# ScalarE's order of the layer-2 copies, GpSimd's order of gathers, TensorE's order of layer-2 pairs, in a three-layer interaction network on one core

## What is computed

```
xk = relu(einsum('bmd,bhd,mhk->bkd', x0, xk, W))     # W0: 32x32x64, W1 and W2: 32x64x64
outs.append(sum(xk, axis=2))
```

## Time and profile before

| | us |
|---|---|
| median of 3 runs | 665.63 |
| lowest, highest | 664.72, 666.06 |
| the profiled execution | 662.89 |
| its span | 661.1 |
| PE busy in the span | 605.5 (92%) |
| DVE busy | 569.6 (86%) |
| POOL busy | 453.1 (69%) |
| ACT busy | 358.0 (54%) |

### The profile page before, as it was taken

How to read it: one execution, slowest core, us unless ns; L and a number is a source line. 1 busy time by engine, 2 the same in 40 slices (tenths; PEclk the granted TensorE clock), 3 DMA queues, 4 the chain that set the end, 5 groups by cost and what they waited for, 6 DMA issues and landing times. The chain is left out here.

```text
span 661.1 us, 9151 instructions
## 1 busy us (share of the span) xinstructions
PE 605.5 (92%) x3172; PEld 247.5 (37%) x3172; DVE 569.6 (86%) x336; ACT 358.0 (54%) x669; POOL 453.1 (69%) x307
## 2 busy tenths in 40 slices
PE   4499849979999999989999999999999999999988
PEld 3352313224343344424343344434443443434434
DVE  5759975986989899897989899898989898999863
ACT  0184922817647392927647392928556482829251
POOL 6786887888869694888869697787877070716220
PEclk9689969989999999999999999999999999999989
DMA  6899679797695969698694969688795869492000
GB/s 186 190 240 278 150 213 214 217 216 193 146 248 142 208 199 214 193 200 237 141 255 137 213 193 211 193 198 225 180 258 131 186 217 217 155 214 41 1 0 1
DMA packets 60175, 119.82 MB, mean 181 GB/s; under 512 B 15271, under 2 KB 33734, under 8 KB 60054
## 3 DMA queue, kind: packets, MB, share of 16 engines
q1 hardware_dynamic: 41798, 111.02, 67.1%
q10 hardware_dynamic: 10768, 6.53, 3.7%
q0 software_dynamic: 7584, 1.96, 3.0%
HBM read 115.27 MB, written 5.25 MB: 182 GB/s over the span
## 5 line engine op out<-in xcount | busy, mean ns | idle before, releaser
L483 DVE TENSOR_TENSOR z_dve<-xq,x0b 128x2048 f32<-128x2048 f32 x209 | 464.5, 2283 | 68.4 <-ACT xq L637 39.2
L879 PE MATMUL acc<-z_dve,w_cin 128*64 128x512 f32 x1672 | 379.2, 597 | 11.1 <-DVE z_dve L483 10.8
L439 POOL TENSOR_TENSOR z_pool<-x0b,xs 128x2048 f32<-128x2048 f32 x47 | 213.5, 4558 | 108.2 <-ACT xs L637 107.2
L423 POOL DMA_INDIRECT emb<-in_tbl_dram,ids_all x224 | 220.0, 982 | 72.0 <-issue 70.3
L879 PEld LDWEIGHTS acc<-z_dve,w_cin 128*64 128x64 f32 x1672 | 122.4, 137 | 234.9 <-issue 186.5
L645 ACT ACTIVATE xq<-acc 32x512 f32<-32x512 f32 x256 | 144.6, 565 | 3.4
L637 ACT ACTIVATE xq<-acc 64x512 f32<-64x512 f32 x128 | 73.0, 570 | 119.8 <-DVE z_dve L483 62.8
L879 PE MATMUL acc<-z_pool,w_cin 128*64 128x512 f32 x376 | 90.6, 615 | 16.1 <-POOL z_pool L439 16.1
L637 ACT ACTIVATE xs<-acc 64x512 f32<-64x512 f32 x128 | 75.7, 591 | 1.9
L483 DVE TENSOR_TENSOR z_dve<-xq,x_rot 128x2048 f32<-128x2048 f32 x30 | 67.2, 2281 | 0.0
L879 PE MATMUL acc<-z_dve,w_sym 128*64 128x512 f32 x256 | 58.0, 593 | 0.2 <-DVE z_dve L483 0.2
(11 more groups left out here) (97 smaller groups left out, 229.2 us busy)
## 6 DMA issues: line engine op xcount, KB each, us to landing
x0b<-x0t SPq DMA_DIRECT2D x120, 512.0 KB, 14.5
x_rot<-x0t SPq DMA_DIRECT2D x60, 512.0 KB, 6.2
x_rep<-x0t SPq DMA_DIRECT2D x15, 512.0 KB
x0b<-x0t SPq DMA_DIRECT2D x16, 256.0 KB, 7.2
emb<-in_tbl_dram,ids_all POOLq DMA_INDIRECT x224
x0t<-emb_t ACTq DMA_DIRECT2D x28, 128.0 KB
w_cin<-in_L_rec_W_dram SPq DMA_DIRECT2D x16, 64.0 KB
x_lo<-x0t SPq DMA_DIRECT2D x15, 64.0 KB
```

What stands on the lines that cost most here:

```text
L423: nc.gpsimd.indirect_dma_start(out=rows[:, D * f:D * f + D], out_offset=None, in_=tables[f], in_offset=bass.IndirectOffsetOnAxis(ap=ids_al ...
L439: nc.gpsimd.tensor_tensor(z_pool[:, n % ZP_SLOTS, :, :], x0b[b % 2][:, 2 * j:2 * j + 2, :], xs[l - 1][:, :].unsqueeze(1).broadcast_to([P, ...
L483: nc.vector.tensor_tensor(z_dve[:, base % Z_SLOTS, :, :], in0.unsqueeze(1).broadcast_to([P, 2, N]), in1, ALU.mult).then_inc(z_made, 1)
L879: ins = nc.tensor.matmul(acc[l][K * side:K * side + K, :], weights[c], z[:, c, NH * side:NH * side + NH], start=start and c == 0, stop=sto ...
```

## The change

ScalarE calls `x2_swp` ahead of `x2_pool` in every block. GpSimd issues 16 gathers ahead of its pair of layer 2 and none behind, in blocks 2 and later; `gathers(0)` and `gathers(1)` keep their numbers. TensorE takes (NAT, 3) of layer 2, GpSimd's pair, seventh and not fifth.

```diff
     def gathers(b):
 
-        return (9, 1, 12) if b == 0 else (0, 14, 8) if b == 1 else (0, 14, 2)
+        return (9, 1, 12) if b == 0 else (0, 14, 8) if b == 1 else (0, 16, 0)
...
     def l2_order(b):
 
-        return [(NAT, 0), (NAT, 1), (NAT, 2), (SWP, 0), (NAT, 3), (SWP, 1), (SWP, 2), (SWP, 3)]
+        return [(NAT, 0), (NAT, 1), (NAT, 2), (SWP, 0), (SWP, 1), (SWP, 2), (NAT, 3), (SWP, 3)]
...
                     x2_nat(t, k)
+                    x2_swp(t, k)
                     x2_pool(t, k)
-                    x2_swp(t, k)
                     if not last:
                         x1_pool(t, k + 1)
```

## The result

| | before | after |
|---|---|---|
| median of the runs, us | 665.85 (4 runs) | 683.63 (4 runs, 679.9 to 685.19) |
| ratio to before, 95% interval | | 1.0268 (1.024 to 1.0296) |
| the profiled execution, us | 662.89 | 685.19 |
| its span, us | 661.1 | 683.4 |

The account below looks back on a forecast made before the run. TensorE bounds the kernel, with its waits deciding; at the start GpSimd's chain does. 7.3 + 2.9 + 0.5 + 2.9 = 13.6 us on the 665.63 us median gives 679.2 us, 2.0% slower; range 671.5 to 683.5 us.

Parts of the forecast that it names:

- The start, +7.3 us: Blocks 0 to 2: later x2_pool delays GpSimd's layer-2 pairs, so TensorE starts 3.66 and another 3.56 us later.
- the slow clock: Behind TensorE's waits for GpSimd: 8 records at granted clock 0.50, said to add nothing in the start.
- Even blocks, +0.58 us: Layer 2: SWP 2 becomes VectorE's third pair, TensorE 0.58 us later; five blocks (2, 6, 8, 10, 12), 2.9 us.
- Odd blocks and the end: Layer 2 waits ahead of SWP 2: odd blocks +0.5 us; last blocks +2.9 us, 1.16 each in 13 and 15.
- Gathers, nothing of their own: Blocks 2 and later: the two moved gathers (2.5 us) fill GpSimd's wait for x2_pool and cost nothing.
- Blocks 4 and 5, 0: TensorE's losses there (0.58 + 0.13 us) go into its 1.81 us wait in block 6 behind GpSimd's stall.
- the slip: Rival, block 6: GpSimd's 2.1 us delay passes through its 8 us stall; 681.3 us, 683 with slow clock; chance 0.27.

Follow-up runs that it names:

- e6: The change plus 11 and 7 extra TensorE matmuls, results thrown away, ahead of layer 1 of blocks 1 and 2; 681.24 us.
- e4: The change, but ScalarE keeps x2_pool ahead of x2_swp in tile 0 (blocks 0 and 1); 674.83 us.
- e2: The kernel before with only TensorE's layer-2 order changed, GpSimd's pair seventh; 676.65 us, ratio 1.0174.
- e3: The kernel before with only the gathers changed, 16 ahead of GpSimd's pair in blocks 2 and later; 665.06 us, ratio 1.0004.
- e5: The change, but TensorE takes GpSimd's layer-2 pair fifth, as before; 684.15 us, ratio 1.0259.
- e1: The kernel before with only ScalarE's swap of x2_swp and x2_pool; 693.66 us, ratio 1.0418.
- e8: The kernel before, but TensorE takes VectorE's four SWP pairs first in layer 1 of blocks 1 and 2; 662.78 us, ratio 0.9957.
- e10: The change with ScalarE's tile 0 as before and GpSimd's layer-2 pair sixth; 789.74 us where the kernel before took 750.59.
- e13: The kernel of e10 run again in another job; 798.24 us where the kernel before took 751.37.
- e17: The kernel of e10 run a third time; 797.45 us where the kernel before took 756.67.
- e9: The change plus three more gathers into an unread buffer behind GpSimd's first 18 of later tiles; 809.59 us where the kernel before took 750.59.
- e11: The kernel of e10 with three of block 5's gathers moved to blocks 3 (two) and 4 (one); 796.99 us where the kernel before took 750.59.
- e14: The kernel of e11 run again; 794.1 us where the kernel before took 751.37.
- e18: The kernel of e11 run a third time; 798.31 us where the kernel before took 756.67.
- e12: The kernel before with the layer-1 order of e8 and the moved gathers of e16; 749.43 us where the kernel before took 750.59.
- e15: The kernel of e12 run again; 750.53 us where the kernel before took 751.37.
- e16: The kernel before with three of block 5's gathers moved to blocks 3 (two) and 4 (one); 760.92 us where the kernel before took 751.37.

## Why the prediction was right or wrong

**The start, +7.3 us: right in mechanism, too small by the clock.** The waits for GpSimd and its idle time for xs came where they were said to, 3.7 us in block 1 and most of the rest in block 2. TensorE's two waits read 10.86 and 6.77 us where 12.4 and 7.5 were written, since layer 2 of blocks 0 and 1 also ended later, under their cover. Wrong was the sentence that the slow clock "adds nothing, since those 8 records run slow already and the second product is late anyway". I took the number of slow records from the trace of before, 8 at each place. With the change it is 16 at both. The ledger has 4.1 us above the forecast there, and 3.5 of them are these two pairs; e6 gets 2.4 us back by keeping TensorE busy. By the medians the start costs less: e4, which has it as before, lies 8.8 us under the change, 1.5 us more than the 7.3, and has one slow second pair itself. In block 2 the slow second pair came in all four traces with the longer wait, and in e2 with a short one; in block 1 it comes and goes with the same wait, and e3, whose start is that of the kernel before, had it too. The Trainium skill, "TensorE: Matmul & The Clock Gate", Part 1, has two levels of the clock, and every window here agrees, with 0.50 or a value on the way up to 1.00; but I had read from it that longer waits cost only their length, and that the runs deny.

**Even blocks, +0.58 us: measured 0.50.** VectorE's gap went and TensorE still lost, by VectorE's pace, as worked out; its three waits read 0.26 us each where 0.36, 0.45 and 0.45 were written. SWP 0 gained 0.46 and not 0.36 us. e2 (+11.5 us for the order alone) supports it from the other side. Whether the seventh place or the swap is to blame is not one or the other: e5 shows that with the swap the fifth place is as bad.

**Odd blocks and the end.** Blocks 7 to 13 took 1.75 us more against 2.1, the last blocks 2.71 against 2.9. TensorE's waits ahead of SWP 2 in blocks 13 and 15 stand where forecast, 0.86 us long where 1.16 was written:

```profile
594.92 1.94 PE L879 MATMUL acc<-z_dve,w_cin 128*64 128x512 f32 x8 [0.86 <-DVE z_dve L483]
...
668.11 1.94 PE L879 MATMUL acc<-z_dve,w_cin 128*64 128x512 f32 x8 [0.86 <-DVE z_dve L483]
```

**Gathers, nothing of their own:** right, e3.

**Blocks 4 and 5, 0: the step that failed.** I let the stall absorb the chain's late start ("if GpSimd's chain does not slip itself") and gave the slip a chance of 0.27 as a rival, at 681.3 us or 683 with the clock. The stall did not absorb it: it is 7.98 to 8.25 us long in all thirteen traces that have it behind the 126th indirect DMA, however late GpSimd comes to it, and the stretch of blocks 5 and 6 is longer in all six traces with the swap. The trace before had one stall, and one stall cannot tell a fixed length from a fixed end; I chose the cheaper reading. The rival's prices were good: 2.1 and 1.7 us on a stretch that the forecast had at 0, against 4.0 us measured, 1.7 of them the clock.

**The range.** Its upper end took in the slip with its clock, but with a start at the bare 7.3 us. In the medians both misses together are 4.4 us (683.63 less 679.2; the forecast started from 665.63, and the kernel before has 665.85 now), which goes over it by 0.1 us; in the two traces they are 8.1 us. How much of the difference is the draw of the profiled executions is not shown; the granted clock of the change's four runs goes from 0.963 in the longest to 0.967 in the shortest.

## What to carry to other kernels

When an engine works without a gap and another waits for it, look at what every step ahead of that chain does to its start; a copy moved by 4.6 us on a third engine cost 3.7 us twice here, while closing the gap of 0.36 us, for which it was moved, brought nothing. An engine that makes pieces in 2.2 us for one that takes them in 1.75 us needs another engine's piece between them, and a place for that piece is good only if the piece is ready by then. And where a chain has no slack, a delay ahead of it should be priced as passing through it, with the clock behind the wait, until a trace shows something that absorbs it.

## What the runs showed of the hardware that I had not expected

- GpSimd stalls once between two indirect DMAs with nothing in the program to wait for: 7.98 to 8.25 us, behind the 126th, in all thirteen traces of the kernel before, the change, e1 to e8, e10, e13 and e17. Another 24 instructions ahead did not move it; other numbers of gathers moved or shortened it (5.5 us behind the 147th in e9, 3.1 to 3.3 us ahead of the 126th in e11, e14 and e18, none over 1 us in e12, e15 and e16). Its cause is open. In the kernel before the 23rd indirect DMA also reads 8.39 us where nearly all others read 0.94.
- Behind a wait, 8 or 16 of TensorE's records ran at the lower clock, at the same place of the program and with waits of like length (in block 1 a second pair of 1.94 us behind 8.74 us of wait, of 3.68 us behind 8.21; in one kernel 1.94 us in e10 and 3.68 us in e13 and e17). The change's four runs spread over 5.3 us.
- On three other chips the kernel before took 750.6 to 756.7 us instead of 665, and the kernel of e10 39 to 47 us more than that. TensorE pauses there with no releaser; TensorE's waits in e17 have the row below (us in total, times, longest; the line is that of all products of layers 0 to 2), and the kernel before, where it took 662.89 us, has no row like it on this line. Whether it is the chips or the time, and why that kernel loses so much more there, was not tried.

```profile
PE acc L882 <- issue: 32.9, 31, 3.8
```
